# Cross-attention with a mixture of experts on one core: queries of four heads made as three blocks of 128 rows, routing weights turned by VectorE

## What is computed

```python
# x: (16, 256, 128), context: (16, 1601, 96)
q = (layernorm(x) @ Wq).reshape(B, Nq, 16, 64).transpose(0, 2, 1, 3)
k, v = (context @ Wk), (context @ Wv)          # likewise in 16 heads of 64
attn = softmax(einsum('bhid,bhjd->bhij', q, k) * 64 ** -0.5)
x = x + (attn @ v) @ Wo + bo
tokens = layernorm(x)
scores = sigmoid(tokens @ router_weight.T)     # 32 experts in 4 groups; 2 groups and in them 4 experts are kept
w = 2.5 * kept_scores / (sum(kept_scores) + 1e-20)
x = x + sum_e w[e] * down_e(silu(gate_e(tokens)) * up_e(tokens)) + shared(tokens)
```

## Time and profile before

| what | value |
|---|---|
| median of three runs | 3230.2 us |
| the profiled execution | 3230.45 us |
| its span, first to last instruction | 3228.5 us |
| TensorE busy | 3192.1 us, 99% |
| VectorE, ScalarE, GpSimd busy | 74%, 63%, 41% |
| mean granted TensorE clock | 0.997 of full |

### The profile page before, as it was taken

The page is one execution under the profiler, slowest core; times in us unless marked ns, Lnnn a source line. Parts: engine busy times, 40 slices in busy tenths (PEclk is TensorE's granted clock), DMA queues, the critical chain, the costliest instruction groups (busy, mean ns, idle before and its releaser), DMA issues.

```text
span 3228.5 us, 40831 instructions
## 1 busy us (share of the span) xinstructions
PE 3192.1 (99%) x15150; PEld 2544.2 (79%) x15150; DVE 2387.4 (74%) x4866; ACT 2022.8 (63%) x2364; POOL 1333.5 (41%) x894
## 2 busy tenths in 40 slices
PE   7999999999999999999999999999999999999999
PEld 6777777778777777778777777777777778777787
DVE  5777777777777777777777777777777777777766
ACT  4666666666666666666666666666666666676555
POOL 5333433344333444334433344333443334225565
PEclk9999999999999999999999999999999999999999
DMA  2000000000000000000000000000000000105553
GB/s 82 1 17 1 17 1 1 17 1 17 1 17 1 17 1 1 17 1 17 1 17 1 17 1 17 1 1 17 1 17 1 17 1 1 40 3 128 119 128 76
DMA packets 26971, 67.49 MB, mean 21 GB/s; under 512 B 3347, under 2 KB 4628, under 8 KB 26388
## 3 DMA queue, kind: packets, MB, share of 16 engines
q1 hardware_dynamic: 26772, 64.87, 7.7%
HBM read 61.72 MB, written 2.62 MB: 20 GB/s over the span
## 4 chain that ended last, share of the span: by engine, by line
PE 96%; DVE 1%; POOL 1%; issue 1%; ACT 0%; DMA 0%; POOLq 0%; SPq 0%; DVEq 0%; ACTq 0%
PE st L586 12%; PE st L589 12%; PE side L528 11%; PE op L599 11%; PE op L605 11%; PE op L602 11%; PE st L592 11%; PE side L622 3%; PE st L720 2%; PE st L722 2%; PE st L721 2%; PE side L521 1%; PE op L613 1%; PE op L616 1%; PE side L523 1%; PE side L522 1%
## 5 line engine op out<-in xcount | busy, mean ns | idle before, releaser
L466 POOL TENSOR_TENSOR p_lo<-p_full,p_hi 128x1024 fp32r<-128x1024 f32 x320 | 819.8, 2562 | 1754.5 <-ACT p_hi L895 1754.5
L1174 DVE TENSOR_REDUCE m_part<-side 128x1 f32<-128x400 f32 x2016 | 1074.4, 570 | 502.9 <-PE side L528 502.8
L892 ACT ACTIVATE p_full<-st 128x1024 f32<-128x1024 f32 x768 | 789.2, 1028 | 877.9 <-PE st L592 846.6
L895 ACT ACTIVATE p_hi<-st 128x1024 fp32r<-128x1024 f32 x768 | 785.0, 1022 | 0.0
L1157 DVE TENSOR_TENSOR p_lo<-p_full,p_hi 128x1024 fp32r<-128x1024 f32 x448 | 546.0, 1219 | 85.1 <-ACT p_hi L895 85.1
L528 PE MATMUL side<-cT_hi,qT_hi 96*128 96x400 f32 x2016 | 554.8, 346 | 0.0
L586 PE MATMUL st<-qT_hi,cT_hi 97*128 97x512 f32 x1664 | 541.7, 406 | 8.7 <-DMA qT_hi<-m_row 7.8
L589 PE MATMUL st<-qT_lo,cT_hi 96*128 96x512 f32 x1664 | 524.3, 396 | 0.0
L599 PE MATMUL op<-p_hi,v_hi 128*97 128x512 f32 x1536 | 487.0, 398 | 1.6 <-DVE p_lo L1157 1.6
L602 PE MATMUL op<-p_lo,v_hi 128*97 128x512 f32 x1536 | 481.1, 394 | 0.0
L605 PE MATMUL op<-p_hi,v_lo 128*97 128x512 f32 x1536 | 481.1, 394 | 0.0
(11 more groups left out here) (173 smaller groups left out, 3097.7 us busy)
## 6 DMA issues: line engine op xcount, KB each, us to landing
w_rep<-w_rows SPq DMA_DIRECT2D x64, 512.0 KB, 6.5
keys_nat<-in_ctx_keys SPq DMA_DIRECT2D x16, 672.0 KB, 6.0
keys_tur<-in_ctx_turned SPq DMA_DIRECT2D x16, 600.4 KB, 4.8
gud_raw<-in_moe_w SPq DMA_DIRECT2D x2, 1152.0 KB, 7.7
out_x<-x SPq DMA_DIRECT2D x8, 256.0 KB, 2.0
x<-in_x SPq DMA_DIRECT2D x1, 1920.0 KB, 13.5
qT_hi<-m_row SPq DMA_DIRECT2D x64, 4.0 KB
oT<-e_row SPq DMA_DIRECT2D x64, 4.0 KB
```

Of the source, the lines that this page charges most:

```text
L466: pool.tensor_tensor(p_lo[:, slot(s), :], p_full[:, s % 2, :], p_hi[:, slot(s), :].bitcast(F32), ALU.subtract).then_inc(s_lo_pool, 1)
L892: act.activation(p_full[0:m, s % 2, :], made, ACT.Exp, scale=SCALE)
L895: act.activation(p_hi[0:m, slot(s), :], made, ACT.Exp, scale=SCALE).then_inc(s_ex, 1)
L1174: dve.tensor_reduce(m_part[:, k % NT, k // NT:k // NT + 1], where[:, 0:MAXW], AX.X, ALU.max).then_inc(s_drain, 1)
```

## The change

**Queries.** The four heads of a group have 4 x 96 = 384 rows of queries, which is three blocks of 128. `A_hi` and `A_lo` are laid out as three blocks of 128 columns for each group of heads: blocks 0 and 1 hold 96 columns of the first two heads and 32 of the last, and so on (`stacked`). TensorE makes the queries as three blocks (nine matmuls of 256 columns with 128 rows out, in place of twelve with 96 rows). Since the fourth head's queries then stand in the last 32 partitions of each block, ScalarE and VectorE lay them apart: five instructions each per group in place of two (`unstacked`). The first Q job holds two blocks, the second one.

**Products of the weights.** Where they are kept at the start, one instruction becomes three.

**Routing weights.** `route_weights` puts them in `w_new` and turns them with a VectorE transpose (32 x 32 blocks) into `w_turned`; TensorE's and ScalarE's part goes. SyncE stores them by batch, four DMAs each, most of them during the attention.

```diff
-        A_hi = sb(att, "A_hi", [P, H, DC], F32R)
-        A_lo = sb(att, "A_lo", [P, H, DC], F32R)
+        A_hi = sb(att, "A_hi", [P, NGB, 3, P], F32R)
+        A_lo = sb(att, "A_lo", [P, NGB, 3, P], F32R)
...
+        DT = DC // 3
+
+        def stacked(tile, n, banks):
+
+            return [(tile[:, n, 0:2, 0:DC], banks[:, :, 0:DC]),
+                    (tile[:, n, 2, 0:DC], banks[:, 0, DC:2 * DC]),
+                    (tile[:, n, :, DC:P], banks[:, 1, DC:2 * DC].rearrange("p (k m) -> p k m", k=3))]
+
+        def unstacked(tile, where, k):
+
+            last = slice(3 * NQ, GQ)
+            if k == 0:
+                return [(tile[0:DC, 0:BANK], where[0:DC, :]),
+                        (tile[0:DT, last], where[DC:P, 0:NQ]),
+                        (tile[DT:2 * DT, last], where[DC:P, NQ:BANK])]
+            return [(tile[0:DC, BANK:3 * NQ], where[0:DC, 0:NQ]),
+                    (tile[2 * DT:DC, last], where[DC:P, 0:NQ])]
...
-            def store_routing(c):
-                sp.wait_ge(s_wk, c + 1)
-                sp.dma_start(w_rows[c], wT[:, c % 2, :]).then_inc(s_wd, 16)
+            def store_routing(batch):
+
+                sp.wait_ge(s_rw, batch + 1)
+                c, first = batch // 2, batch % 2 * 2 * P
+                for run in range(4):
+                    rows = w_rows[c, :, first:first + 2 * P].rearrange("e (t r j) -> e t r j", t=2, r=4)
+                    sp.dma_start(rows[:, :, run, :],
+                                 w_turned[run * E:(run + 1) * E, batch % 2, :].rearrange("e (t j) -> e t j", t=2)).then_inc(s_wd, 16)
...
+                    if i == NGB - 1 and b >= 2:
+                        store_routing(b - 2)
                     send_max_row(jobs_at(g)["T"][0] + 1, (i + 1) % 2)
...
             def project_queries(where, g, half, k):
-                for h in range(2):
-                    head = g * GH + 2 * k + h
-                    o = where[0:DC, h * NQ:(h + 1) * NQ]
-                    pe.matmul(o, A_hi[:, head, :], x_hi[:, half, :], start=True, stop=False)
-                    pe.matmul(o, A_hi[:, head, :], x_lo[:, half, :], start=False, stop=False)
-                    mm = pe.matmul(o, A_lo[:, head, :], x_hi[:, half, :], start=False, stop=True)
+                for block in ((0, 1), (2,))[k]:
+                    o = where[:, block % 2 * NQ:(block % 2 + 1) * NQ]
+                    pe.matmul(o, A_hi[:, g, block, :], x_hi[:, half, :], start=True, stop=False)
+                    pe.matmul(o, A_hi[:, g, block, :], x_lo[:, half, :], start=False, stop=False)
+                    mm = pe.matmul(o, A_lo[:, g, block, :], x_hi[:, half, :], start=False, stop=True)
                 mm.then_inc(s_fill, 1)
...
-            def turn_routing(c, where):
-                for t in range(4):
-                    mm = pe.transpose(where[0:E, t * P:(t + 1) * P], w_all[:, 4 + c * 4 + t, :], ident[:, :])
-                mm.then_inc(s_wf, 1)
...
-                act.activation(qT_hi[slot][0:DC, k * BANK:(k + 1) * BANK], where[0:DC, :], ACT.Copy).then_inc(s_qh, 1)
+                for into, made in unstacked(qT_hi[slot], where, k):
+                    ins = act.activation(into, made, ACT.Copy)
+                ins.then_inc(s_qh, 1)
...
-            def keep_routing(c, where):
-                act.wait_ge(s_wf, c + 1)
-                if c >= 2:
-                    act.wait_ge(s_wd, 16 * (c - 1))
-                act.activation(wT[:, c % 2, :], where[0:E, :], ACT.Copy).then_inc(s_wk, 1)
...
-                cols = slice(k * BANK, (k + 1) * BANK)
-                dve.tensor_tensor(qT_lo[slot][:, cols], where[0:DC, :], qT_hi[slot][0:DC, cols].bitcast(F32),
-                                  ALU.subtract).then_inc(s_drain, 1)
+                high = unstacked(qT_hi[slot], where, k)
+                for (into, made), (kept, _) in zip(unstacked(qT_lo[slot], where, k), high):
+                    ins = dve.tensor_tensor(into, made, kept.bitcast(F32), ALU.subtract)
+                ins.then_inc(s_drain, 1)
...
-                dve.scalar_tensor_tensor(w_all[:, tiles, :], ra[:, :, :], ROUTE_SCALE, share, ALU.mult,
-                                         ALU.mult).then_inc(s_rw, 1)
+                link(dve.scalar_tensor_tensor(w_new[:, :].rearrange("p (t e) -> p t e", t=2), ra[:, :, :], ROUTE_SCALE,
+                                              share, ALU.mult, ALU.mult))
+                if batch >= 0:
+                    if batch >= 2:
+                        dve.wait_ge(s_wd, 64 * (batch - 1))
+                    dve.transpose(w_turned[:, batch % 2, :], w_new[:, :]).then_inc(s_rw, 1)
```

More of the change, by code:

```diff
@@ L67, in xattn_moe @@
         x2T = sb(stack, "x2T", [P, (B + 1) * NQ])
-        w_all = sb(stack, "w_all", [P, T + 4, E])
-        wT = sb(stack, "wT", [E, 2, BANK])
+        w_new = sb(stack, "w_new", [P, 2 * E])
+        w_turned = sb(stack, "w_turned", [P, 2, 2 * E])
         w_rep = [sb(stack, "w_rep0", [P, 4, BANK])]
@@ L122, in xattn_moe @@
             aw = sb(early, "aw", [P, H // 2, 448])
-            A_raw = sb(early, "A_raw", [P, H, DC])
+            A_raw = sb(early, "A_raw", [P, NGB, 3, P])
         p_full = sb(att, "p_full", [P, 2, GQ])
@@ L167, in xattn_moe @@
         s_ls = sem("router_exponentials_kept")
-        s_rw = sem("routing_weights_kept")
+        s_rw = sem("routing_weights_turned")
         s_ab = sem("weight_products_made")
@@ L344, in _ @@
             turns(body)
-            store_routing(0)
             spread_routing(0, 0)
+            store_routing(B - 3)
             sp.wait_ge(s_oe, NG)
@@ L350, in _ @@
             for c in range(NCH - 1):
-                store_routing(c + 1)
                 for part in range(4):
@@ L356, in _ @@
                         store_output(c - 1)
+                if c == 1:
+                    store_routing(B - 2)
+                    store_routing(B - 1)
             for c in (NCH - 2, NCH - 1):
@@ L690, in body @@
                     pv(t - 2)
-                    if g == NG - 1 and t == 2:
-                        pe.wait_ge(s_drain, first_job[g])
-                        pe.wait_ge(s_rw, B)
-                        turn_routing(0, bank(first_job[g] + 1))
                     side_jobs(at[t][1])
@@ L782, in _ @@
                         turn_output(c - 1)
-                    if q == 2 and c + 1 < NCH:
-                        if c:
-                            pe.wait_ge(s_wk, c)
-                        else:
-                            pe.wait_ge(s_drain, JOBS_END)
-                        if c + 1 == NCH - 1:
-                            pe.wait_ge(s_rw, B + 2)
-                        turn_routing(c + 1, side[:, (c + 1) % 2, :])
             for g in range(NCH * NP - 3, NCH * NP):
@@ L821, in keep_products @@
                     act.wait_ge(s_ab, 2 * n + 2)
-                    act.activation(four_heads(A_raw, n), products(banks, slice(0, 2 * DC)), ACT.Copy)
-                    act.activation(four_heads(A_hi, n), products(banks, slice(0, 2 * DC)), ACT.Copy)
+                    for tile in (A_raw, A_hi):
+                        for into, made in stacked(tile, n, banks):
+                            act.activation(into, made, ACT.Copy)
                 b = B_all[0:DC, 4 * n:4 * n + 4, 0:D].rearrange("p (c j) m -> p j c m", c=2)
@@ L829, in _ @@
             act.wait_ge(s_ab, 2)
-            act.activation(four_heads(A_hi, 0), products(op, slice(0, 2 * DC)), ACT.Copy).then_inc(s_xh, 1)
+            for into, made in stacked(A_hi, 0, op):
+                ins = act.activation(into, made, ACT.Copy)
+            ins.then_inc(s_xh, 1)
             act.wait_ge(s_tur, 16)
@@ L913, in body @@
                         x2_hi_of(0)
-                    if g == NG - 1 and s == 3:
-                        keep_routing(0, bank(first_job[g] + 1))
                     extra = EXTRA.get(i, {}).get(s)
@@ L966, in _ @@
                         hidden_hi(g - 1)
-                    if q == 3 and c + 1 < NCH:
-                        keep_routing(c + 1, side[:, (c + 1) % 2, :])
                     if g == 10:
@@ L1098, in strike, with route_weights @@
                 link(ins)
-            def route_weights(tiles):
+            def route_weights(batch):
                 link(dve.tensor_tensor(ra[:, :, :], struck[:, :, 0:E], choice[:, :, 0:E], ALU.not_equal))
@@ L1118, in _ @@
             dve.wait_ge(s_xh, 2)
-            first = A_hi[:, 0:4, :].rearrange("p (c j) m -> p j c m", c=2)
-            dve.tensor_tensor(A_lo[:, 0:4, :].rearrange("p (c j) m -> p j c m", c=2),
-                              op[:, :, 0:2 * DC].rearrange("p j (c m) -> p j c m", c=2), first.bitcast(F32),
-                              ALU.subtract).then_inc(s_Al, 1)
+            for (into, made), (kept, _) in zip(stacked(A_lo, 0, op), stacked(A_hi, 0, op)):
+                ins = dve.tensor_tensor(into, made, kept.bitcast(F32), ALU.subtract)
+            ins.then_inc(s_Al, 1)
             for k in range(2):
@@ L1214, in late_steps @@
                     elif i == 2:
```

(6 more changed lines are left out.)

13 lines of the change are left out of this document (3 added, 10 removed).

## The result

The changed kernel took 3319.85 us (median of 4 runs, 3315.25 to 3325.45), the kernel before on the same chip 3230.27 us (4 runs). The ratio is 1.0284, 95% interval 1.0271 to 1.0296: slower by 2.8%. The forecast was 3325 us. The profiled execution took 3315.25 us, span 3313.5 us, mean granted clock 0.995.

The account below looks back on a forecast made before the run. It took a ScalarE and VectorE chain at each group's end to bound the kernel. Terms 87.3 + 8.5 - 3.5 + 0.6 + 1.2 = 94.1 us on 3230.45 us gave 3325 us, range 3305 to 3345 (chance 0.55).

Parts of the forecast that it names:

- The bound: Group ends: a ScalarE and VectorE chain as long as TensorE's work, slack 0.07 us, hides the matmuls saved (23 us).
- TensorE idles for over 1.5 us, 62 times: Sign of being right: TensorE idles that long in front of step 2's scores or `weigh_half`, 62 times.
- Held pieces on both engines: Query laying: pieces changing start partition wait for the one ahead; half step's `exp` +0.98 us, VectorE's early steps +1.59.
- What reaches the next group: Lengthening at group ends: 1.38, 1.59, 1.09, 1.56 us for first to fourth group, 87.3 us in all.
- TensorE's clock: Attention groups: TensorE's added idling lets its clock fall five times at 1.7 us, 8.5 us; bounds none and 105 us.
- Routing: Experts' part: 3.5 us gained from TensorE's dropped transposes, 0.6 us lost in the second chunk to VectorE's transpose.
- Start: Before the first maxima: more copies of products and queries cost 1.2 us, bounds 0 and 3.
- The chain is not what binds: Rival: laying fits in ScalarE's and VectorE's idle time, TensorE gains 23 us, 3204 us; faster or no change, chance 0.08.
- Pieces overlap: Rival: laying pieces overlap as ordinary neighbours do on both engines, 39 us added, 3267 us; chance 0.12.
- Only one engine holds: Rival: pieces wait on one engine only; VectorE alone some 70 us, 3299, ScalarE alone some 60 us, 3289; chance 0.15.
- The clock falls in most groups: Rival: TensorE's clock falls in half of 62 groups, 53 us in place of 8.5, 3369 us, up to 3420; chance 0.10.

Follow-up runs that it names:

- e2: The kernel before with nine query matmuls a group in place of twelve, three heads leaving out the hi by lo product: 3225.33 us against 3228.14.
- e3: The changed kernel with the fourth head's pieces read from and written to partition 0 on both ScalarE and VectorE: 3260.11 us, ratio 1.0097 to the kernel before.
- e4: The changed kernel with only ScalarE's pieces of the fourth head read from and written to partition 0: 3299.67 us, ratio 1.0219 to the kernel before.
- e8: The changed kernel with only VectorE's pieces of the fourth head read from and written to partition 0: 3284.00 us, ratio 1.0166 to the kernel before.
- e7: The changed kernel, `exp(0)` not waiting for VectorE's last `lo` of a group, most laying behind that `lo`, late routing steps at steps 4 and 6: 3272.04 us.
- e1: The kernel before with only the routing weights turned on VectorE, nothing else of the change: 3226.21 us against 3228.14, ratio 0.9989.
- e10: The changed kernel, most laying behind VectorE's last `lo` of a group, `exp(0)` still waiting for it, late steps singly behind steps 3 to 9: 3287.68 us.
- e6: The changed kernel, most laying behind VectorE's last `lo` of a group, late steps at steps 4 and 6, `exp(0)` still waiting for that `lo`: 3296.90 us.
- e9: The changed kernel, `exp(0)` not waiting for VectorE's last `lo`, most laying behind that `lo`, late steps singly behind steps 3 to 9: 3260.63 us.

## Why the prediction was right

The profiled executions differ by 3315.25 - 3230.45 = 84.8 us; the sum was 94.1.

- **The bound.** Right. That TensorE's 99% hides a chain of the same length was read from the group without Q jobs; e2 shows it: 23 us of matmuls are worth 3. The sign "TensorE idles for over 1.5 us, 62 times" was not met in size: by the profile it idles 0.85 us in front of `qk(2)` in all 62 groups and 0.33, 0.57, 0 and 0.49 us in front of `weigh_half` by group, so 0.85 to 1.42 us.
- **Held pieces on both engines.** Right, and shown by e3, e4 and e8. `exp` of the half step at 3.24 us (step: 3.29), early steps at 4.95 (4.98).
- **What reaches the next group.** Right: +1.30, +1.56, +1.11, +1.51 us by group, in place of 1.38, 1.59, 1.09, 1.56. The first half's copy stands at 86.28 us (before 84.14), that of the last group but one at 2965.40 (2877.31 in rows 8): the 62 periods grew by 88.09 - 2.14 = 85.95 us, of which one fall of the clock is 1.5; the term was 87.3.
- **TensorE's clock.** Over-sized for the profiled execution: 8.5 us for five falls of 1.7, where one more than before stands in the attention and costs 1.5 (a group of 48.22 us in place of 46.71, near 331 us). TensorE's row there, and behind it the stretch around it (columns as for e7):

```profile
330.58 1.04 PE L610 MATMUL st<-qT_hi,cT_hi 97*128 97x512 f32 x2 [0.87 <-ACT p_hi L896]
```

```profile
330.00:334.00 4.00, 3.42 (x9) 0.60 0.00 0
```

  Most groups idle in just this way, in two stretches of 0.3 to 0.6 and 0.85 us, and keep the upper level (2.4 GHz). The other runs of the changed kernel took 3318.5 to 3325.5 us with a mean clock of 0.995 to 0.993, so more falls in them are likely, but not shown. If so, that is why the median came nearer to the forecast than the profiled execution: by an estimate from these clocks, 0.002 of 3320 us is 6.6 us.
- **Routing.** Right in sum: by their spans the two executions differ by 3313.5 - 3228.5 - 88.1 = -3.1 us behind the last group but one, with the last group 0.2 of it (terms -3.5 and +0.6). The changed one has a fall of the clock more there (at 3010 and 3089 us, before at 2922 alone), so that by an estimate without it the gain is 4 to 5 us. e1 measured -1.9 us, with an interval of -0.6 to -6.5. The transpose is 0.245 us (taken 0.3 with its wait).
- **Start.** Under-sized: 2.1 us in place of 1.2, within its bounds of 0 and 3. Only a part of that is the new layout. TensorE also stands at the lower clock for longer there: until 51.0 us, in the kernel before until 48.3. Two runs part the two, by an estimate: the lower clock ends at 49.3 us in e2 and, with the new layout, at 49.8 in e10, and the first half's copy stands at 84.28 and 85.74 us. So the layout makes some 1.4 us of the 2.1, near the term, and the rest goes with the clock.
- **Rivals.** "The chain is not what binds" (3204) fell with e2. "Pieces overlap" (3267) is no state of this kernel, but its price was good: made to overlap (e3), the kernel takes 3260. "Only one engine holds" gave 3289 for ScalarE alone and 3299 for VectorE alone; e8 and e4 make these cases, and measured 3284 and 3300. "The clock falls in most groups" (3369) fell with the profiled execution: one fall more than before in 62 groups.

Of the 9.3 us between the sum and the profiled executions some 7 are the clock and 2.9 the ends of the groups (87.3 against 86.0 less one fall), with 0.9 of the start against them. That the median lies within 5.2 us of the forecast is in part luck: it has to do with the other runs' clocks. The forecast was right for its reasons; the expectations of e6, e7 and e9 were not. They went wrong for the most part by one thing, that a step of VectorE was priced by its own row and not by what GpSimd does when it is issued. The 448 `lo` of the kernel before show no trace of it, they lie within 16 ns. But its experts' part does, and there it was overlooked. Timeline of the kernel before, GpSimd and VectorE:

```profile
2977.39 1.29 POOL L481 TENSOR_TENSOR h_lo<-hid,h_hi 128x512 fp32r<-128x512 f32 x1 [0.77 <-ACT h_hi L944]
2977.48 1.23 DVE L1082 TENSOR_SCALAR g_keep<-g_keep 128x8 f32<-128x8 f32 x1
```

The step of 8 columns, 0.17 us elsewhere, takes 1.23 and ends 0.03 us after GpSimd's instruction.

## What to carry to other kernels

A busy share of 99% doesn't say that the engine binds: look for a place where it has less to do than usual, as the last group but one here, and see whether the next point comes earlier. Price a split of one instruction into several by the start partition of each piece, on ScalarE as on VectorE, and by what waits behind the last of them; put the pieces behind the instruction that others wait for. When small VectorE steps are moved, look first at what GpSimd runs at the new place.

## What the runs showed of the hardware that was not expected

- ScalarE holds an instruction that starts at another partition, as VectorE does (the prediction had one row for it): a distance of 0.39 us in place of 0.26 between copies of 256 columns (changed kernel and e3), worth 20 us of the kernel on ScalarE alone (3319.9 to 3299.7, e4) and 36 on VectorE alone (to 3284.0, e8).
- A VectorE step of 8 columns takes 1.4 us in place of 0.17 if it is issued while GpSimd's 2.6 us `lo` runs, and a `lo` of VectorE 3.08 in place of 1.22 (e9, e7). GpSimd waits likewise: its cast takes 1.51 us in place of 0.51 beside that `lo` (e7). The maxima from PSUM (L1197, L1184) beside GpSimd's `lo` kept their 0.57 us.
- The same waits of TensorE in each group, up to 0.87 us long, let its clock fall once in the attention of the profiled execution; idling of 1.4 us once in four groups (e7) was met by a fall in 8 of 15 such places and a mean clock of 0.991.
